# A graph layer and an expert layer in one kernel: the folded weights are applied before the masked sum instead of after it

## The reference, cut to what matters

```python
# x: 4096 x 256 f32; adj: 4096 x 4096 int32
def gnn(z, adj):                       # z = layernorm(x)
    mask = (adj > 0)
    agg = mask @ z / max(sum(mask, axis=1), 1)
    combined = concat([z @ W_self + b_self, agg @ W_nb + b_nb])
    return relu(combined @ W_comb + b_comb)
x = x + gnn(layernorm(x), adj)
x = x + ffn(layernorm(x))              # 8 experts, 2 per token: gelu(x @ W1 + b1) @ W2 + b2
```

## Time and profile before

| | |
|---|---|
| median of 3 runs | 521.37 us (521.02 to 539.54) |
| the profiled execution | 522.74 us |
| its span | 520.9 us |
| PE / DVE / ACT / POOL busy | 435.4 / 390.0 / 270.7 / 298.6 us |
| moved by DMA | 122.49 MB, mean 235 GB/s |

### The profile page before, as it was taken

How to read it: one execution, slowest core, us unless ns; L and a number is a source line. 1 busy time by engine, 2 the same in 40 slices (tenths; PEclk the granted TensorE clock), 3 DMA queues, 4 the chain that set the end, 5 groups by cost and what they waited for, 6 DMA issues and landing times.

```text
span 520.9 us, 13160 instructions
## 1 busy us (share of the span) xinstructions
PE 435.4 (84%) x4322; PEld 384.9 (74%) x4322; DVE 390.0 (75%) x1209; ACT 270.7 (52%) x427; POOL 298.6 (57%) x306
## 2 busy tenths in 40 slices
PE   0337899699999999999999999982799999998720
PEld 0225789598978999899898988971598889996610
DVE  5759766676487888788688888867777787789982
ACT  3654444354346363364356445333288888886630
POOL 3897223243345665666666566356766678785570
PEclk9976999799999999999999999996699999999985
DMA  9987999999979999999999996461676556589565
GB/s 251 258 269 171 242 270 315 242 272 276 241 180 263 297 248 265 283 257 277 276 286 276 295 272 176 115 204 62 225 221 179 169 170 187 166 303 376 196 211 163
DMA packets 47121, 122.49 MB, mean 235 GB/s; under 512 B 9033, under 2 KB 18125, under 8 KB 46032
## 3 DMA queue, kind: packets, MB, share of 16 engines
q1 hardware_dynamic: 29584, 68.28, 50.6%
q0 software_dynamic: 16080, 50.49, 31.0%
q10 hardware_dynamic: 1392, 2.88, 1.9%
HBM read 96.52 MB, written 26.93 MB: 237 GB/s over the span
## 4 chain that ended last, share of the span: by engine, by line
PE 29%; DVE 27%; DMA 15%; issue 13%; ACT 7%; POOL 4%; DVEq 2%; SPq 1%; POOLq 0%; ACTq 0%
PE bank L1166 8%; PE bank L1167 8%; DMA stage<-in_adj_dram,gidx 8%; PE bank L1175 4%; DVE rows L1081 4%; DMA wst<-in_L_ffn_W_dram 4%; PE bank L1284 3%; PE bank L1304 3%; DVE mask L800 2%; DMA x_sb<-in_x_dram 2%; DVE maskT L807 2%; ACT aT L684 2%; ACT mask L649 2%; DVEq L388 1%; POOL stage L557 1%
## 5 line engine op out<-in xcount | busy, mean ns | idle before, releaser
L1166 PE MATMUL bank<-z_flat,maskT 128*128 128x257 f16 x1024 | 231.3, 277 | 13.0 <-DVE maskT L807 13.0
L1167 PE MATMUL bank<-z_lo,maskT 128*128 128x256 f16 x1024 | 231.1, 276 | 0.0
L1166 PEld LDWEIGHTS bank<-z_flat,maskT 128*128 128x128 fp8e4 x1024 | 101.5, 99 | 26.8 <-POOL z_lo L583 12.4
L557 POOL DMA_INDIRECT stage<-in_adj_dram,gidx x64 | 66.3, 1036 | 80.2 <-PE bank L1175 41.9
L622 POOL DMA_INDIRECT pair_out<-rows,enum x78 | 87.7, 1124 | 40.4 <-issue 18.2
L1167 PEld LDWEIGHTS bank<-z_lo,maskT 128*128 128x128 fp8e4 x1024 | 101.2, 99 | 12.6
L678 ACT ACTIVATE rows<-bank,rdeg 128x256 f16<-128x256 f32 x32 | 15.1, 473 | 134.9 <-DVE rdeg L869 134.9
L568 POOL DMA_INDIRECT dispatched<-rows,slot x64 | 64.3, 1005 | 26.2 <-issue 17.5
L649 ACT ACTIVATE mask<-stage,m 128x2048 fp8e4<-128x2048 int32 x32 | 64.5, 2014 | 20.7 <-DMA stage<-in_adj_dram,gidx 20.7
L606 POOL TENSOR_TENSOR rs<-ve,mhalf 128x1 f32<-128x1 f32 x32 | 42.4, 1326 | 51.1 <-DVE ve L893 50.9
L1284 PE MATMUL bank<-stage,w 128*128 128x256 f16 x468 | 60.2, 280 | 5.4 <-DVE stage L1073 5.3
(11 more groups left out here) (183 smaller groups left out, 629.4 us busy)
## 6 DMA issues: line engine op xcount, KB each, us to landing
stage<-in_adj_dram SPq DMA_DIRECT2D x128, 256.0 KB, 8.3
stage<-dispatched SPq DMA_DIRECT2D x39, 260.0 KB, 2.9
wst<-in_L_ffn_W_dram SPq DMA_DIRECT2D x16, 256.0 KB
z_lo<-pair_out SPq DMA_DIRECT2D x4, 1024.0 KB, 7.7
dispatched<-pad SPq DMA_DIRECT2D x15, 260.0 KB, 16.0
out_dram<-x_sb SPq DMA_DIRECT2D x28, 128.0 KB
maskT<-pair_out SPq DMA_DIRECT2D x3, 1024.0 KB, 9.0
x_sb<-in_x_dram SPq DMA_DIRECT2D x6, 256.0 KB, 11.5
```

What stands on the lines that cost most here:

```text
L557: gp.indirect_dma_start(out=stage[:, s, b - 2, :], out_offset=None, in_=adj_q[:, :], in_offset=bass.IndirectOffsetOnAxis(ap=gidx[:, 0:1], ...
L1166: mm(acc[u % 2][:, 0:D + 1], a, z_hi[:, i, :], start=(i == 0), stop=False)
L1167: last = mm(acc[u % 2][:, 0:D], a, z_lo[:, i, :], start=False, stop=(i == NT - 1))
```

## The change

The product with the folded weights moves from behind the masked sum to ahead of it: `mask @ (z W)` in place of `(mask @ z) W`. Degree and scale are divided out afterwards.

- **Set-up.** The rows are normalised in f32 into the row buffers `rows` (8 tiles by ACT, 24 by POOL). A loop over 16 pairs of tiles follows: PE transposes both tiles in f32 (4 transposes, run 5 pairs ahead), ACT and DVE copy them as high and low f16 part (`zT`), PE multiplies with the neighbour half and then the own half of `wf` (12 matmuls each), ACT and DVE split the neighbour product into `z_hi` and `z_lo`, and ACT scales the own product back into the row buffer, where POOL adds the constant row. Masks of tiles 0 to 3 are made inside this loop (ACT at pairs 3, 6, 9, 12, DVE at 4, 7, 10, 13), and statistics of groups 4 to 7 at pairs 0, 2, 4, 6.
- **Main loop.** Per step, 8 transposes, 12 product matmuls, the copy L684, the split L678/L876 and their waits are gone. Once the masked sum of a tile is there, DVE divides it by degree and scale, adds the waiting row, and goes on; the lags shrink by two steps.
- **DMA order.** The weights and `Wg` are requested ahead of most of x; the 15 dummy blocks are written after the last masks instead of in steps 4 to 18.

```diff
-        AGG, EVAC, X1, NORM, LOGIT, SCORE, HOT, SLOT = 3, 4, 5, 6, 7, 8, 11, 13
-        PA, PZ, PT, PL, PR = 1, 2, 4, 5, 10
+        X1, NORM, LOGIT, SCORE, HOT, SLOT = 3, 4, 5, 6, 9, 11
+        PT, PL, PR = 2, 3, 8
-        OWN = 24
+        OWN, PAIRS, AHEAD = 2 * B, NT // 2, 5
+        MASK_A, MASK_D = (3, 6, 9, 12), (4, 7, 10, 13)
+        FIRST = len(MASK_A)
 # SP
-            for i in range(3):
-                load_x(sp, i, (0, 1))
+            load_x(sp, 0, (0, 1))
             for w, m in enumerate((W_self, W_nb)):
                 sp.dma_start(wraw[:, w], ...).then_inc(s_w, 16)
+            sp.dma_start(wg_f[:, :, :], ...)
+            load_x(sp, 1, (0, 1))
...
                 load_adj(t)
-                if 4 <= t < 4 + DUM:
-                    write_dummy(t - 4)
             sp.wait_ge(s_tab, 2)
             sp.wait_ge(s_mA, NT)
             sp.wait_ge(s_mD, NT)
+            sp.wait_ge(s_pad, 2)
+            for i in range(DUM):
+                write_dummy(i)
 # POOL
+            def self_and_const(k):
+                if k == 0:
+                    pool.wait_ge(s_cb, 1)
+                pool.wait_ge(s_self, 2 * k + 2)
+                gp.tensor_tensor(rows_f[:, at(B * k, B), 0:D], rows_f[:, at(B * k, B), 0:D], const_bc[...], ALU.add)
+            for k in range(NG):
+                rstd(k)
+                if k >= OWN // B:
+                    pool.wait_ge(s_nb, k + 1)
+                    for t in range(B * k, B * k + B):
+                        normalise(t)
+                if k in (2, 3):
+                    gather(k - 2)
+            pool.dma_start(b1c[:, :, :], ...)
+            self_and_const(0)
+            gather(2)
+            self_and_const(1)
+            self_and_const(2)
+            gather(3)
+            self_and_const(3)
+            gather(4)
...
-                if s + 2 < NT:
+                if FIRST <= s < NT - 2:
                     gather(s + 2)
 # ACT
+            for i in range(PAIRS):
+                act.wait_ge(s_up, i + 1)
+                sc.activation(z_hi[:, at(2 * i, 2), 0:D], pair(ups[i % 2]), ACT.Copy, scale=UNIT).then_inc(s_uh, 1)
+                act.wait_ge(s_sp, i + 1)
+                sc.activation(rows_f[:, at(2 * i, 2), 0:D], pair(sps[i % 2]), ACT.Copy, scale=scw[:, 2:3]).then_inc(s_self, 1)
+                if i + AHEAD < PAIRS:
+                    zt_hi(i + AHEAD)
+                if i in MASK_A:
+                    masks(t, t, t)          # t = MASK_A.index(i)
 # DVE
+            stats(0)
+            stats(1)
             dve.wait_ge(s_small, 16 * 5)
...
+            for i in range(PAIRS):
+                if i in (0, 2, 4, 6):
+                    stats(NG // 2 + i // 2)
+                dve.wait_ge(s_uh, i + 1)
+                v.scalar_tensor_tensor(z_lo[:, at(2 * i, 2), :], pair(ups[i % 2]), UNIT, z_hi[...], ALU.mult, ALU.subtract)
+                if i + AHEAD < PAIRS:
+                    zt_lo(i + AHEAD)
+                if i in MASK_D:
+                    masks(t, t, t)          # t = MASK_D.index(i)
+                    mask_transpose(t, t, t)
 # DVE, main step
+                    dve.wait_ge(s_mm, j + 1)
+                    v.tensor_scalar(sdeg[...], p[:, D:D + 1], 1.0, scw[:, 4:5], ALU.max, ALU.mult)
+                    v.reciprocal(rdeg[...], sdeg[...])
+                    dve.wait_ge(s_sfc, j // B + 1)
+                    v.scalar_tensor_tensor(tsum[...], p[:, 0:D], rdeg[...], x_row(j), ALU.mult, ALU.add)
 # PE
+            for i in range(PAIRS):
+                pe.wait_ge(s_ztl, i + 1)
+                if i >= 2:
+                    pe.wait_ge(s_ul, i - 1)
+                    pe.wait_ge(s_self, i - 1)
+                for ps, cols, done in ((ups[i % 2], slice(D, 2 * D), s_up), (sps[i % 2], slice(0, D), s_sp)):
+                    for t in range(2):
+                        last = product(ps[:, t * D:t * D + D], ...)      # 6 matmuls, 256 columns
+                    last.then_inc(done, 1)
+                if i + AHEAD < PAIRS:
+                    z_transpose(i + AHEAD)
 # PE, main step: product(zb, ...) twice and the 8 transposes into etp16[0] are removed
```

More of the change, by code:

```diff
@@ L83, in gnn_moe_kernel @@
         tps = bank[2:4]
-        zb = bank[4][:, 0:D]
+        ups, sps = bank[4:6], bank[6:8]
         tp2 = bank[5][:, 0:D].bitcast(F16)
@@ L650, in masks @@
                               saturate=False).then_inc(s_mA, 1)
[L652 to L668, removed]
@@ L669, in _, with normalise, zt_hi @@
-            masks(1, 1, 1)
-            act.wait_ge(s_scw, 1)
+            def normalise(k):
+                act.wait_ge(s_nb, k + 1)
+                for t in range(B * k, B * k + B):
+                    sc.activation(x_row(t), flat(x_sb, t), ACT.Identity, bias=nbx[:, at(t)], scale=rs[:, at(t)]).then_inc(s_xhA, 1)
+            def zt_hi(i):
+                act.wait_ge(s_ztp, i + 1)
+                if i >= ZR:
+                    act.wait_ge(s_sp, i - ZR + 1)
+                sc.copy(zT[:, i % ZR, 0].rearrange("p q n -> p (q n)"), tps[i % 2][:, :]).then_inc(s_zth, 1)
@@ L671, in _ @@
+            for w in range(2):
+                act.wait_ge(s_wtp, w + 1)
+                sc.copy(wT[:, w].rearrange("p t n -> p (t n)"), wps[w][:, :]).then_inc(s_wtc, 1)
+            for k in range(OWN // B):
+                normalise(k)
+            for i in range(AHEAD - 1):
+                zt_hi(i)
+            act.wait_ge(s_scw, 2)
             for w in range(KT):
                 sc.activation(wf[:, 0, w, :], fold[w][:, :], ACT.Copy, scale=scw[:, 0:1]).then_inc(s_wfh, 1)
-            def main_step(t, u, known):
[L675 to L684, removed]
+            zt_hi(AHEAD - 1)
@@ L694, in main_step @@
                     sc.copy(row16[:, at(t - NORM), 0:D].rearrange("p o d -> p (o d)"), xh[:, (u - NORM) % 2, :]).then_inc(s_hi2, 1)
-                if live(known, 0) and known not in (0, 1):
+                if live(known, 0) and known >= FIRST:
                     masks(t, u, known)
@@ L788, in _, with stats @@
             v.memset(cmin[:, 0:1], 0.0).then_inc(s_cst, 1)
-            for k in range(NG):
+            def stats(k):
                 if k in XCUT:
@@ L827, in _ @@
             v.tensor_reduce(fmx[:, 1:2], wg_f[:, :, :].rearrange("p t n -> p (t n)"), AX.X, ALU.max, apply_absolute_value=True).then_inc(s_fmx, 1)
[L828 to L839, removed]
+            stats(2)
+            zt_lo(0)
+            zt_lo(1)
+            fold_max(0)
+            stats(3)
+            zt_lo(2)
+            fold_max(1)
+            zt_lo(3)
             dve.wait_ge(s_fmr, 1)
@@ L1144, in _, with fold_weights @@
                 last.then_inc(s_wtp, 1)
-            pe.wait_ge(s_wtc, 2)
-            for dt in range(KT):
+            def fold_weights(dt):
                 for w in range(2):
```

180 lines of the change are left out of this document (81 added, 99 removed).

## The result

The changed kernel is **slower**: 549.69 us median of 4 runs (546.39 to 553.66), the kernel before beside it 522.07 us; ratio 1.053, 95% interval 1.047 to 1.059. Two more measurements of the same kernel, on other chips, gave 1.048 (1.043 to 1.053) and 1.036 (1.023 to 1.049). Forecast were 517 us and a range of 498 to 532. Ratios and intervals leave out executions more than 1.5% above the fastest of their kernel; medians count all. The profiled execution took 546.39 us with a span of 544.6, 28.4 us above the 516.2 of the sum.

What follows compares the result with a forecast made beforehand. PE and DMA were both taken to bound the main loop, with DMA setting the end after the change: last sum 6.7 us later, tail 11.4 us shorter, net -4.7, giving 517 us; range 498 to 532.

Steps and rivals of the forecast that it cites:

- Small loads land at 22.6 us: Set-up: last small load issued behind x at 9.52 us, landing 13.1 us later, as before.
- Pair 0: Set-up: the first pair of products on PE starts at 37.5 us, after loads, statistics, low parts, scale chain and split.
- The pair at 3.59 us: Pair loop on PE: 24 matmuls, 2.63 us, plus 4 f32 transposes, 0.96 us; eleven pairs at 3.59 us.
- 2 us of waits: Pair loop: DVE's work, under PE's 52.6 us but bunched at pairs 4 to 7, costs 2 us of waits.
- First sum: End of the pair loop: first masked sum starts at 94 us, with 0 to +7 us if tile 2's gather is late.
- Load of tile 6 at 112 us: Main loop's start: this load waits for mask 4, behind DVE's reading of tile 1's sum, until 112 us.
- Rate 281 GB/s: Main loop: DMA moves the remaining 63.3 MB at 281 GB/s, bounds 257 and 296, in 225 us.
- From the last adjacency to the last sum 10.7 us: Main loop's end: ACT's mask 2.0, transposition 1.25, 64 matmuls 7.0, handing over 0.4; last sum ends at 349.7 us.
- Dummies cost nothing: After the last mask: 15 dummy blocks, 4.0 MB, take 13.5 us ahead of dispatched reads; cost 0, or 3 us at 205 GB/s.
- Tail 12.9 us: Last sum to last placing: 12.9 us, 11.4 gained; bounds 6 (choice for second last group in the way) to 13.
- The rival of the slow pair loop: Pair loop at DVE's and POOL's pace: DVE's 39 us become 68, sum starts at 109, total 532 us; chance 0.15.
- PE would set the end: Main loop rival: DMA gives more when asked, so PE ends the loop at 331 us; total 498 us; chance 0.20.

Runs made afterwards that it cites:

- the fewer bytes: Changed kernel with a quarter of the adjacency's bytes not loaded from tile 6 on: 0.981 of the kernel before; the same cut in the kernel before: 0.989.
- the fastest kernel: Changed kernel with masks 0 to 6 made in the pair loop, later ones up to 4 steps ahead, and the old load order: 514.37 us, 0.979 of before.

## Why the prediction was wrong, step by step

The mechanism was the forecast one (the transfers set the end, PE's shorter step turns into waits); its terms were too small, nearly all on the same side. The steps that failed are two above all: the start of tile 6's load, put at 112 us and measured at 122.9, and the way from the last adjacency to the last sum, put at 10.7 us and measured at about 19. They are 20 of the 28 us. Term by term, against the forecast span of 516.2 us:

- **Small loads land at 22.6 us: wrong, 29.05.** The step took the earlier trace rows's 13.1 us because "all of x was ahead of it before, too". The diff also put the weights ahead of x, in packets under 2 KB. In the first 10 us the engines served 1583 packets, 1347 of them under 2 KB, where before they served 828, 316 under 2 KB; at 202 against 222 GB/s. From 10 to 20 us it was 215 against 305. With the old load order the landing is back at 22.88 us; that it is the packets' size and not their place in the queue is my reading. Moving a step means pricing what it moves past, and here it was x. Pair 0: 43.75 for 37.5 us, **+6.3**.
- **The pair at 3.59 us: too long.** The pairs came 3.07 us apart (43.75 to 46.82): four transposes behind one another cost 0.44 us, not 4 x 0.24 from the earlier trace rows. Over the eleven pairs that have transposes it gave 5.8 us back, and that was luck: two errors of opposite sign.
- **"2 us of waits" in the loop: wrong.** The gather of tile 2 stood on GpSimd behind normalising, a 1.9 us load issue and a sum of 2.38 us, and ACT's mask, ahead of ACT's evacuations in order, held the pairs for 8.20 us. The text had it as "0 to +7" and took 0. Waits and low clock took 9.1 us together, for 4. First sum 99.63 for 94: **+5.6** net of the three.
- **Load of tile 6 at 112 us: wrong, 122.9.** Beside the 5.6, mask 4 stands on DVE behind the expert scales of step 3, which wait 8.07 us for a matmul in the middle of PE's step 2. The sum had mask 4 behind the reading of tile 1's sum alone. **+5.3**. Together the load is 10.9 us late, and from there it counts in full.
- **Rate 281 GB/s: nearly right.** 279 from 160 to 320 us at share 1.04; last adjacency 230 us after its start, for 227. **+3**.
- **From the last adjacency to the last sum 10.7 us: wrong, about 19.** I counted one tile's way. But ACT's mask 31 waits for DVE's rows, not for its load, so the transposed mask is ready at 359.87 us, 6.4 us behind the load and not 3.7; and PE is then still in step 30, since its steps 29 to 31 follow one another, and begins sum 31 near 365.9 us. **+9**.
- **Dummies cost nothing: right, but their number was wrong.** Seven are written, not 15: they are issued from 363.19 to 368.93 us, for a forecast 13.5 us from 341, and the reads of dispatched rows start at 370.87 us. With the seven back in the loop those reads start at 365.30 us and the time is the same.
- **Tail 12.9 us: 16.2.** Tile 31's sum is read only at 375.91 us, behind the choice for group 6, which was the lower bound's reason. Gain over before 8 us, not 11.4. **+3.3**, and 2.1 in the phase behind it, whose cause is open.

10.9 + 3 + 9 + 3.3 + 2.1 = 28.3 us, the whole miss of 28.4. The rival of the slow pair loop gave 532 us through contention on DVE and POOL. It priced the late start at 15 us, where 10.9 were measured, but its cause was not the one: in the changed kernel no DVE mask ran above 1.41 us, and the one row of GpSimd that a mask held up lost 0.9 us. That PE would set the end was refuted by the fewer bytes. And the range took its two upper bounds, 100 us for the first sum and 265 GB/s, one at a time; both together give some 536 us, and the way from the last adjacency to the last sum had no bound at all. Waits between engines that work in a fixed order only ever delay here, and they add up.

## What to carry to other kernels

When an edit moves work ahead of a loop that consumes a stream, count the bytes that can still flow while the moved work runs, with the buffers there are: here six of 32 tiles, and 42 us of idle transfers undid more than the shorter steps could give. Then let the consumer of the stream (the conversion that frees its buffers) run ahead of the arithmetic, with as many small buffers as the memory lends for a while. And when bytes are cut and a busy engine's waits vanish with no other edit, the engine named in those waits was only passing a delay on.

## What the runs showed of the hardware

- **GpSimd and VectorE block each other, in one case for 4 us.** In the fastest kernel, VectorE's mask, 1.23 us alone, took 5.25 and 4.26 us when it was issued inside the first of two back-to-back sums of GpSimd; it ended 1.1 us after the second:

```profile
70.42 4.70 POOL L595 TENSOR_TENSOR rows<-rows,const_bc 128x1024 f32<-128x1024 f32 x2
94.06 4.69 POOL L595 TENSOR_TENSOR rows<-rows,const_bc 128x1024 f32<-128x1024 f32 x2
```
```profile
70.96 5.25 DVE L818 TENSOR_SCALAR mask<-stage 128x2048 fp8e4<-128x2048 int32 x1
95.58 4.26 DVE L818 TENSOR_SCALAR mask<-stage 128x2048 fp8e4<-128x2048 int32 x1 [1.76 <-issue]
```

  The Trainium skill (SBUF — State Buffer, "Who interferes with whom") says that VectorE in a two-port mode contends with GpSimd, and that the one that issues first has the shared port pair for its whole instruction while the other fully blocks. These rows agree, and the mask waited longer than one instruction: the second sum, too, went ahead of it. The other way round, in the changed kernel, GpSimd's first row of a group was issued inside a mask and took 1.46 us instead of 0.55:

```profile
61.00 1.22 DVE L815 TENSOR_SCALAR mask<-stage 128x2048 fp8e4<-128x2048 int32 x1
61.18 1.46 POOL L581 TENSOR_SCALAR rows<-x_sb,rs,w 128x256 f32<-128x256 f32 x1
```

- GpSimd normalised 128x256 f32 in 0.54 us (four in 2.16) and added 128x1024 in 2.36 us, a little under the 0.69 and 2.76 taken for them.
- The kernel before took 522 to 523 us on some chips and 543 to 549 us on others; the changed kernel's ratio to it moved less, 1.036 to 1.053. In the traces the difference lies behind the last sum: from its end to the end of the span the changed kernel took 172 us on the chip with 522 us, and with the old load order 190 us on the chip with 543 us, where the DMA engines moved 165 GB/s from 382 to 500 us against 215.
